# One helper of a fused attention and FFN block moved behind the attention core

## The chip, the cores and the metric

The kernel runs as one program on 8 NeuronCores of a Trainium2 chip. The metric is the device time in microseconds (us) of the slowest core. The engines are named as in the profile: PE is the matrix engine (PEld its weight load), DVE the vector engine, ACT the scalar engine, POOL the engine that issues the software DMAs here, and SP the engine that issues the DMA transposes. SPq, ACTq and POOLq are their queues of issued DMAs.

## The reference

A "macaron" block over x of shape (4, 4096, 1024), with 16 heads of 64:

```python
x = x + 0.5 * ffn(layernorm(x))
x = x + attn(layernorm(x))      # q, k with rotary embedding, |i - j| <= 128, softmax, Wo
x = x + 0.5 * ffn(layernorm(x))
# ffn: xr, xk mix x with the row before; sigmoid(xr @ W_r) * (relu(xk @ W_k)**2 @ W_v)
# rope: (x0, x1) -> (x0*c - x1*s, x1*c + x0*s), position modulo 256
```

Each core computes 2048 of the 16384 rows, with some rows of its neighbours added at either end.

## The kernel before

A core holds 20 tiles of 128 rows. Stage 1 is the first FFN, then comes the attention stage, then stage 4, the second FFN; x is spilled to the DRAM tensor `xscr` between them. The helper `P.op` appends an instruction with its semaphore waits to the list of one engine, so that every engine works through its own list in the order in which the Python code emits it, and nothing reorders them.

The attention stage is a loop over j = 1 to 19 in `emit_attn_stage`. One turn emits, in this order:

- `emit_qkv(j)`: 54 matmuls of 512 columns (L601, L606) into two PSUM banks in turn, and six copies on ACT (L625) into `qaug`, `kaug` and `vaug`. `qaug` and `kaug` exist once.
- `emit_qkv_tail(j)`, below called the tail: on ACT a square of q (L636), on DVE a sum per head (L642) and a maximum (L647), on ACT a logarithm and an exponential (L649, L651), on DVE the product that fills a 65th column of `qaug` (L655). This is the norm of q, which serves as stabilizer of the softmax. Then six DVE operations turn q and k in place (the rotary embedding, "rope": L667, L672 and L677, first for q, then for k). At the end SP transposes `qaug` into `qpl` and `kaug` into `kpl`.
- `emit_attn_core(j - 2)`, from j = 4 on: for each head three score matmuls (L709), an exponential on ACT (L718), a mask product on DVE (L723), and two heads later three matmuls with v (L736), evacuated by ACT or DVE in turn (L746, L751). Two PSUM banks hold scores. At its end DVE divides by the row sums (16 operations, L767), and SP transposes the result into `attnfm`.
- `emit_ln2(j + 1)`: the layer norm of the next tile: two passes over x on ACT (L204, L207), small operations on DVE and ACT, the scaled tile on DVE (L234), and a transpose on SP into `ln2fm`, for which the matmuls of `emit_qkv(j + 1)` wait.
- `emit_wo(j - 3)`, from j = 5 on: 18 matmuls (L789, L794) and two additions to x on DVE (L800), a store to `xscr` on POOL, and then the load of tile j + 5.

Turn j = 6 puts three large copies on POOL behind its store: W_r, W_k and W_v of the FFN are cast to 16 bits from DRAM to DRAM (`ffn16`). After turn 19 ACT issues three loads of these weights into `warena`, and then attention core 18, `emit_wo(17)` and `emit_wo(18)` close the stage.

Attention core j - 2 needs the transposes of tiles up to j - 1 only, not those of the tail of its own turn.

Of the kernel before, what the change touches and what calls it, by code (L numbers as in the profile page):

```python
# [11 lines left out]
ALU = mybir.AluOpType  # L12
AX = mybir.AxisListType
AP = bass.AP

NH, HD, DM = 16, 64, 1024
# [50 lines left out]
def build_nc():  # L67
# [34 lines left out]
    C_sb = sb("C_sb", [128, 2, DM], F16)  # L102
    S_sb = sb("S_sb", [128, 2, DM], F16)
    Cq_sb = sb("Cq_sb", [128, 2, DM], F16)
    Sq_sb = sb("Sq_sb", [128, 2, DM], F16)
# [15 lines left out]
    qsq_free = {0: []}  # L121
    qsq_waw = []
# [3 lines left out]
    P = Prog(nc)  # L126
# [16 lines left out]
    for hf, snw in ((0, "gw0a"), (1, "gw0b")):  # L143
        P.op("g", GD(warena[:, :, 512 * hf:512 * (hf + 1)],
                     AP(wr_d.tensor, 512 * hf, [[DM, 128], [128 * DM, 8], [1, 512]])),
             incs=[(snw, 16)])
# [5 lines left out]
    for nmw, (i, wd) in (("gw1", (1, wk_d)), ("gw2", (2, wv_d))):  # L152
# [5 lines left out]
         incs=[("gwo", 16)])  # L158
# [16 lines left out]
    v_cq = P.n("v")  # L175
# [329 lines left out]
    def emit_attn_stage(barrier, t_s1_mm, t_s1, s1_slots, s1_spill):  # L505
# [127 lines left out]

        def emit_qkv_tail(j):
            ev1, ev3 = qkv_ev[j]
            P.op("a", lambda a: a.activation(qsq[:, :],  # L636
                                             AP(qaug, 0, [[2 * DM, 128], [128, NH], [1, 64]]),
                                             AF.Square),
                 waits=[("s", ev1)] + qsq_free[0] + qsq_waw[:], incs=[("s", 1)])
            qsq_waw[:] = [("s", P.n("s"))]  # L640
            s_sq = P.n("s")
            P.op("v", lambda v: v.tensor_reduce(qm[:, 0, :],  # L642
                                                qsq[:, :].rearrange("p (h d) -> p h d", h=NH),
                                                AX.X, ALU.add),
                 waits=[("s", s_sq)], incs=[("v", 1)])
            qsq_free[0] = [("v", P.n("v"))]
            P.op("v", lambda v: v.tensor_scalar(qm[:, 0, :], qm[:, 0, :], 1e-12, None, ALU.max),  # L647
                 fence=True, incs=[("v", 1)])
            P.op("a", lambda a: a.activation(qm[:, 1, :], qm[:, 0, :], AF.Ln),  # L649
                 waits=[("v", P.n("v"))], incs=[("s", 1)])  # L650
            P.op("a", lambda a: a.activation(qm[:, 1, :], qm[:, 1, :], AF.Exp, scale=0.5),  # L651
                 waits=[("s", P.n("s"))], incs=[("s", 1)])
            s_nrm = P.n("s")
            with nc.allow_low_precision(reason="stabilizer M col; any nearby value is valid"):
                P.op("v", lambda v: v.tensor_tensor(  # L655
                    AP(qaug, 64, [[2 * DM, 128], [128, NH], [1, 1]]),
                    qm[:, 1, :], nkb2b[:, :], ALU.mult),
                    waits=[("s", s_nrm), ("v", v_pre)], incs=[("v", 1)])
            m_tok = P.n("v")
            par2 = (j + 1) % 2  # L660
            rope_tok = {}
            for which, aug, evw in (("q", qaug, ev1), ("k", kaug, ev3)):
                CC = Cq_sb if which == "q" else C_sb
                SS = Sq_sb if which == "q" else S_sb
                dv = AP(aug, 0, [[2 * DM, 128], [128, NH], [1, 64]])
                sv = AP(aug, 32, [[2 * DM, 128], [128, NH], [-32, 2], [1, 32]])
                P.op("v", lambda v, dv=dv, par2=par2, CC=CC: v.tensor_tensor(  # L667
                    t1[:, :].rearrange("p (h d) -> p h d", h=NH), dv, CC[:, par2, :]
                    .rearrange("p (h d) -> p h d", h=NH), ALU.mult),
                    waits=[("s", evw)] + ([("v", v_cq)] if which == "q" else []),  # L670
                    fence=(which == "k"), incs=[("v", 1)])
                P.op("v", lambda v, sv=sv, par2=par2, SS=SS: v.tensor_tensor(  # L672
                    t2[:, :].rearrange("p (h b d) -> p h b d", h=NH, b=2), sv,
                    SS[:, par2, :].rearrange("p (h b d) -> p h b d", h=NH, b=2), ALU.mult),
                    incs=[("v", 1)])
                w = [("s", s_sq)] if which == "q" else []
                P.op("v", lambda v, dv=dv: v.tensor_tensor(  # L677
                    dv, t1[:, :].rearrange("p (h d) -> p h d", h=NH),
                    t2[:, :].rearrange("p (h d) -> p h d", h=NH), ALU.add),
                    waits=w, fence=True, incs=[("v", 1)])  # L680
                rope_tok[which] = P.n("v")
            sn = f"yt{j % 4}"
            P.op("y", YT(qpl[:, j % 4, :, :], qaug[:, :]),
                 waits=[("v", rope_tok["q"]), ("v", m_tok)] + qpl_free[j % 4] +
                       ([(sn, P.n(sn))] if P.n(sn) > 0 else []),
                 incs=[(sn, 16)])
            P.op("y", YT(kpl[:, j % 4, :, :], kaug[:, :]),
                 waits=[("v", rope_tok["k"])] + kpl_free[j % 4], incs=[(sn, 16)])
            tr_tok[j] = (sn, P.n(sn))
# [129 lines left out]
        emit_ln2(1)  # L819
        for j in range(1, NT):  # L820
            emit_qkv(j)
            emit_qkv_tail(j)
            if QT0 <= j - 2 <= QT1:
                emit_attn_core(j - 2)
            if j + 1 < NT:
                emit_ln2(j + 1)
            if j == 1 or j == 19:
# [146 lines left out]
```

How the kernel before makes its waits and increments, by code:

```python
    def replay(self, q, eng, sems):  # L55
        for waits, build, incs in self.qs[q]:
            for s, v in waits:
                eng.wait_ge(sems[s], v)
            inst = build(eng)
            for s, a, _ in incs:
                if inst is None:
                    eng.sem_inc(sems[s], a)
                else:
                    inst.then_inc(sems[s], a)
```

## Time and profile before

| what | value |
|---|---|
| median of 2 runs | 1639.91 us (1636.69 to 1643.13) |
| the profiled execution, its own time | 1641.2 us |
| its span, slowest core (of 1620.9 to 1639.6) | 1639.6 us |
| PE busy | 1005.4 us, 61% |
| DVE busy | 610.3 us, 37% |
| ACT busy | 496.9 us, 30% |
| mean granted PE clock of the two dies | 0.771 and 0.743 |

No engine is busy all the time. The attention stage runs from about 486 us to about 1330 us of the span. In the rows below an instruction stands with its start and duration in us, and in brackets the idle time of its engine before it and what ended it.

### The profile page before, as it was taken

The page shows a single profiled execution, that of the slowest core. Times are in us where ns is not written, and L with a number is a line of the kernel's source. Part 1 is how long each engine was busy: PE and PEld are TensorE (multiplying, and loading weights), DVE is VectorE, ACT ScalarE, POOL GpSimd, SP SyncE. Part 2 cuts the span into 40 slices and gives each one's busy share as a digit, 9 for nine tenths or more (in the row PEclk, how much of TensorE's full clock was granted, in tenths as well). Part 3 has the DMA queues.
Part 4 walks back from the last instruction along what each step waited for, and adds up shares of the span by engine and source line. Part 5 has one row for each costly group of instructions (what it writes and reads, how often), then busy time and mean ns, then how long its engine had stood idle before and what let it go on. Part 6 is the DMA issues. An engine that isn't in the chain of part 4 may idle for free.

```text
span 1639.6 us, 18625 instructions; the slowest of 8 cores (1620.9 to 1639.6 us)
## 1 busy us (share of the span) xinstructions
PE 1005.4 (61%) x4645; PEld 427.0 (26%) x4645; DVE 610.3 (37%) x1674; ACT 496.9 (30%) x1054; POOL 38.4 (2%) x71
## 2 busy tenths in 40 slices
PE   0067842877816466662766766777766735767576
PEld 0023311332302122221333322333333312323222
DVE  1074403445311333332333333333344425445542
ACT  0133220432112233331333333333333422342231
POOL 1000000000010000000000000000000010000000
PEclk9987765777757766775777777777777766888878
DMA  9914495331381222269122232222222472333221
GB/s 149 208 33 102 104 114 118 89 90 52 90 275 33 44 47 40 65 92 165 31 61 65 65 63 53 54 65 52 52 52 52 107 238 48 90 95 86 71 71 65
DMA packets 224373, 141.16 MB, mean 86 GB/s; under 512 B 195472, under 2 KB 197648, under 8 KB 224080
## 3 DMA queue, kind: packets, MB, share of 16 engines
q1 hardware_dynamic: 193088, 48.25, 15.6%
q0 software_dynamic: 16592, 50.08, 15.1%
q10 hardware_dynamic: 14592, 41.63, 7.3%
q8 instruction: 45, 0.74, 0.2%
q14 instruction: 56, 0.46, 0.1%
HBM read 86.47 MB, written 39.85 MB: 77 GB/s over the span
## 4 chain that ended last, share of the span: by engine, by line
PE 36%; DVE 22%; DMA 18%; issue 9%; ACT 7%; SPq 4%; ACTq 1%; DVEq 1%; POOL 0%; POOLq 0%
PE pb L601 15%; PE pb L401 7%; DMA ln_fm_s<-ln_tm 7%; PE pb L709 4%; DMA ln2fm_s<-ln_tm 4%; SPq L137 4%; PE pb L736 3%; DVE xkm_s L346 3%; PE pb L369 3%; DVE xrm_s L341 3%; DMA kfm_s<-kpre_s 3%; PE pb L606 2%; DVE attn_tm_s L767 2%; ACT qsq L207 2%; DVE ln_tm L234 2%
## 5 line engine op out<-in xcount | busy, mean ns | idle before, releaser
L601 PE MATMUL pb<-warena,ln2fm_s 128*128 128x512 f16 x912 | 246.1, 418 | 165.0 <-DMA ln2fm_s<-ln_tm 165.0
L401 PE MATMUL pb<-warena,kfm_s 128*128 128x512 f16 x560 | 171.7, 476 | 155.7 <-DMA kfm_s<-kpre_s 154.6
L369 PE MATMUL pb<-warena,xrm_s 128*128 128x512 f16 x560 | 146.9, 423 | 107.9 <-DVE stats L211 50.3
L642 DVE TENSOR_REDUCE qm_s<-qsq 128x16 f32<-128x1024 f16 x19 | 23.2, 1220 | 401.3 <-ACT qsq L636 401.3
L709 PE MATMUL pb<-qpl_s,kpl_s 65*128 65x128 f16 x816 | 121.6, 286 | 73.4 <-ACT probsT_s L718 72.1
L601 PEld LDWEIGHTS pb<-warena,ln2fm_s 128*128 128x128 f16 x912 | 85.8, 104 | 292.4 <-issue 227.8
L718 ACT ACTIVATE probsT_s<-pb 128x384 bf16<-128x384 f32 x272 | 131.4, 490 | 50.6 <-PE pb L709 45.4
L369 PE MATMUL pb<-warena,xkm_s 128*128 128x512 f16 x560 | 140.2, 409 | 0.0
L736 PE MATMUL pb<-vaug_s,probsT_s 128*128 128x65 f16 x816 | 90.3, 236 | 78.2 <-DVE probsT_s L723 64.6
L401 PEld LDWEIGHTS pb<-warena,kfm_s 128*128 128x128 f16 x560 | 64.2, 117 | 259.9 <-issue 243.4
L379 ACT ACTIVATE r_sb_s<-pb 128x512 f16<-128x512 f32 x70 | 38.9, 595 | 274.0 <-DVE xr_sb L414 138.2
L204 ACT ACTIVATE ln_tm<-xr_sb 128x1024 f16<-128x1024 f32 x56 | 58.9, 1052 | 189.8 <-DVE xr_sb L414 56.4
L723 DVE TENSOR_TENSOR probsT_s<-probsT_s,gates_sb 128x256 bf16<-128x256 bf16 x272 | 76.4, 291 | 93.4 <-ACT probsT_s L718 66.7
L369 PEld LDWEIGHTS pb<-warena,xrm_s 128*128 128x128 f16 x560 | 58.3, 106 | 192.3 <-issue 164.8
L625 ACT ACTIVATE qaug_s<-pb 128x512 f16<-128x512 f32 x38 | 22.7, 597 | 228.0 <-PE pb L606 228.0
L789 PE MATMUL pb<-warena,attnfm_s 128*128 128x512 f16 x272 | 89.4, 488 | 3.8 <-DMA attnfm_s<-attn_tm_s 2.2
L736 PEld LDWEIGHTS pb<-vaug_s,probsT_s 128*128 128x128 bf16 x816 | 56.5, 117 | 121.4 <-issue 119.4
L709 PEld LDWEIGHTS pb<-qpl_s,kpl_s 65*128 65x128 f16 x816 | 62.9, 116 | 94.6 <-issue 83.5
L369 PEld LDWEIGHTS pb<-warena,xkm_s 128*128 128x128 f16 x560 | 57.9, 103 | 76.3 <-issue 44.0
L336 DVE TENSOR_TENSOR d_fm_s<-ln_fm_s 128x2048 f16<-128x2048 f16 x18 | 22.2, 1234 | 138.4 <-DMA ln_fm_s<-ln_tm 138.4
L409 DVE SCALAR_TENSOR_TENSOR t_sb_s<-pb,r_sb_s 128x512 f32<-128x512 f32 x70 | 47.0, 687 | 59.9 <-PE pb L401 59.9
L234 DVE TENSOR_SCALAR ln_tm<-xr_sb,stats 128x1024 f16<-128x1024 f32 x56 | 43.9, 810 | 48.7 <-ACT stats L228 48.7
(82 smaller groups left out, 842.4 us busy)
## 6 DMA issues: line engine op xcount, KB each, us to landing
xr_sb<-xscr POOLq DMA_DIRECT2D x36, 512.0 KB, 4.5
xr_sb<-x ACTq DMA_DIRECT2D x20, 512.0 KB, 5.4
xscr<-xr_sb ACTq DMA_DIRECT2D x19, 512.0 KB, 2.9
xscr<-xr_sb POOLq DMA_DIRECT2D x17, 512.0 KB, 2.9
out<-xr_sb ACTq DMA_DIRECT2D x16, 512.0 KB, 2.6
wqkv<-wqkv POOLq DMA_DIRECT2D x1, 6144.0 KB, 59.0
warena<-wqkv ACTq DMA_DIRECT2D x3, 2048.0 KB, 29.8
warena<-ffn ACTq DMA_DIRECT2D x3, 2048.0 KB, 21.5
```

Source lines behind the costliest of these rows:

```text
L137: YT = lambda o, i: (lambda y: y.dma_start(o, i, transpose=True))
L204: P.op("a", lambda a: a.activation(ln_tm[:, par, :], x_ap, AF.Copy, accum_out=sl(0)), waits=list(waits) + lnT_free[par] + stats_free.pop(s ...
L234: P.op("v", lambda v: v.tensor_scalar(ln_tm[:, par, :], x_ap, sl(2), sl(5), ALU.subtract, ALU.mult), waits=[("s", stok)] + list(waits) + l ...
L341: P.op("v", lambda v, c=c, gp=gp, o=o: v.scalar_tensor_tensor(xrm2[:, gp, c, o:o + 256], d_fm[:, c, o:o + 256], negmu[:, c:c + 1], ln_fm[: ...
L369: t.matmul(pb[bk][:, :], xm[:, gp, c, 128 * ti:128 * (ti + 1)], warena[:, c, woff + 512 * js:woff + 512 * (js + 1)], start=(c == 0), stop= ...
L401: P.op("t", lambda t, bk=bk, c=c, pp=pp, js=js: t.matmul(pb[bk][:, :], kfm[:, pp, c, :], warena[:, c, 2 * DM + 512 * js:2 * DM + 512 * (js ...
L601: P.op("t", lambda t, bk=bk, c=c, par=par, js=js: t.matmul(pb[bk][:, :], ln2fm[:, par, c, :], warena[:, c, 512 * js:512 * (js + 1)], start ...
L709: P.op("t", lambda t, sl=sl, h=h, ci=ci, par=par, bk=bk_sc: t.matmul(pb[bk][:, ci * 128:(ci + 1) * 128], AP(kpl, sl * NH * 128 + h * 128, ...
L718: P.op("a", lambda a, h=h, bk=bk_sc, hp=hp: a.activation(probsT[:, hp, :], pb[bk][:, 0:384], AF.Exp), waits=[("t", sc_tok[(i, h)])] + wp, ...
L723: P.op("v", lambda v, hp=hp, gi=gi: v.tensor_tensor(AP(probsT, hp * 384, [[4 * 384, 128], [256, 2], [1, 128]]), AP(probsT, hp * 384, [[4 * ...
L736: P.op("t", lambda t, sl=sl, h=h, ci=ci, hp=hp, bk=bk_pv: t.matmul(pb[bk][:, 0:65], AP(probsT, hp * 384 + ci * 128, [[4 * 384, 128], [1, 1 ...
L789: P.op("t", lambda t, bk=bk, c=c, par=par, js=js: t.matmul(pb[bk][:, :], attnfm[:, par, c, :], warena[:, c, 3 * DM + 512 * js:3 * DM + 512 ...
```

## The change

The tail is emitted behind the attention core of its turn instead of ahead of it. Inside the tail the rope of q and k comes first, and the norm of q is taken of the turned q (a turn leaves the norm as it is), so the square waits for the rope of q instead of for the copies from PSUM. No instruction is added or taken away.

```diff
         def emit_qkv_tail(j):
             ev1, ev3 = qkv_ev[j]
+            par2 = (j + 1) % 2
+            rope_tok = {}
+            for which, aug, evw in (("q", qaug, ev1), ("k", kaug, ev3)):
...
+                P.op("v", lambda v, dv=dv: v.tensor_tensor(
+                    dv, t1[:, :].rearrange("p (h d) -> p h d", h=NH),
+                    t2[:, :].rearrange("p (h d) -> p h d", h=NH), ALU.add),
+                    fence=True, incs=[("v", 1)])
+                rope_tok[which] = P.n("v")
             P.op("a", lambda a: a.activation(qsq[:, :],
                                              AP(qaug, 0, [[2 * DM, 128], [128, NH], [1, 64]]),
                                              AF.Square),
-                 waits=[("s", ev1)] + qsq_free[0] + qsq_waw[:], incs=[("s", 1)])
+                 waits=[("v", rope_tok["q"])] + qsq_free[0] + qsq_waw[:], incs=[("s", 1)])
...
-            par2 = (j + 1) % 2
-            rope_tok = {}
-            for which, aug, evw in (("q", qaug, ev1), ("k", kaug, ev3)):
...
             sn = f"yt{j % 4}"
             P.op("y", YT(qpl[:, j % 4, :, :], qaug[:, :]),
-                 waits=[("v", rope_tok["q"]), ("v", m_tok)] + qpl_free[j % 4] +
+                 waits=[("v", m_tok)] + qpl_free[j % 4] +
                        ([(sn, P.n(sn))] if P.n(sn) > 0 else []),
                  incs=[(sn, 16)])
...
         for j in range(1, NT):
             emit_qkv(j)
-            emit_qkv_tail(j)
             if QT0 <= j - 2 <= QT1:
                 emit_attn_core(j - 2)
+            emit_qkv_tail(j)
             if j + 1 < NT:
                 emit_ln2(j + 1)
```

On ACT, at the end of a turn and the start of the next, before (`vaug_s<-pb` is the last copy of the QKV product, `probsT_s` an exponential of the attention core, `ln_tm` and `qsq<-xr_sb` the two passes of the layer norm):

```order
L718 ACTIVATE probsT_s<-pb 128x384
L746 ACTIVATE attn_un_s<-pb 128x65
L204 ACTIVATE ln_tm,stats<-xr_sb 128x1024
L207 ACTIVATE qsq,stats<-xr_sb 128x1024
L227 ACTIVATE stats<-stats 128x1
L228 ACTIVATE stats<-stats 128x1
L625 ACTIVATE qaug_s<-pb 128x8x64 x2
L625 ACTIVATE kaug_s<-pb 128x8x64 x2
L625 ACTIVATE vaug_s<-pb 128x8x64 x2
L636 ACTIVATE qsq<-qaug_s 128x1024
L649 ACTIVATE qm_s<-qm_s 128x16
L651 ACTIVATE qm_s<-qm_s 128x16
```

The same stretch now (the code has moved by some lines: L717 and L745 are the old L718 and L746; L657, L670 and L672 are the square, logarithm and exponential of the tail):

```order
L717 ACTIVATE probsT_s<-pb 128x384
L745 ACTIVATE attn_un_s<-pb 128x65
L657 ACTIVATE qsq<-qaug_s 128x1024
L670 ACTIVATE qm_s<-qm_s 128x16
L672 ACTIVATE qm_s<-qm_s 128x16
L204 ACTIVATE ln_tm,stats<-xr_sb 128x1024
L207 ACTIVATE qsq,stats<-xr_sb 128x1024
L227 ACTIVATE stats<-stats 128x1
L228 ACTIVATE stats<-stats 128x1
L625 ACTIVATE qaug_s<-pb 128x8x64 x2
L625 ACTIVATE kaug_s<-pb 128x8x64 x2
L625 ACTIVATE vaug_s<-pb 128x8x64 x2
```

The three operations of the tail have moved from behind the copies of the QKV product to ahead of the layer norm's two passes.

On DVE, from the division at the end of an attention core to the masks of the next, before:

```order
L767 TENSOR_SCALAR attn_tm_s<-attn_un_s,zs_s 128x64 x16
L211 TENSOR_SCALAR stats<-stats 128x1
L218 TENSOR_SCALAR stats<-stats 128x1
L234 TENSOR_SCALAR ln_tm<-xr_sb,stats 128x1024
L800 TENSOR_TENSOR xr_sb<-pb,xr_sb 128x512 x2
L642 TENSOR_REDUCE qm_s<-qsq 128x16
L655 TENSOR_TENSOR qaug_s<-qm_s,nkb2b 128x16
L667 TENSOR_TENSOR t_s<-qaug_s,Cq_sb 128x1024
L677 TENSOR_TENSOR qaug_s<-t_s 128x16x64
L677 TENSOR_TENSOR kaug_s<-t_s 128x16x64
L723 TENSOR_TENSOR probsT_s<-probsT_s,gates_sb 128x2x128 x4
```

The same now (L766 is the old L767, L643 and L652 the old L667 and L677, L663 and L676 the old L642 and L655, L722 the old L723):

```order
L766 TENSOR_SCALAR attn_tm_s<-attn_un_s,zs_s 128x64 x16
L643 TENSOR_TENSOR t_s<-qaug_s,Cq_sb 128x1024
L652 TENSOR_TENSOR qaug_s<-t_s 128x16x64
L652 TENSOR_TENSOR kaug_s<-t_s 128x16x64
L663 TENSOR_REDUCE qm_s<-qsq 128x16
L676 TENSOR_TENSOR qaug_s<-qm_s,nkb2b 128x16
L211 TENSOR_SCALAR stats<-stats 128x1
L218 TENSOR_SCALAR stats<-stats 128x1
L234 TENSOR_SCALAR ln_tm<-xr_sb,stats 128x1024
L799 TENSOR_TENSOR xr_sb<-pb,xr_sb 128x512 x2
L722 TENSOR_TENSOR probsT_s<-probsT_s,gates_sb 128x2x128 x4
```

The whole tail now stands between the division and the statistics of the layer norm, and nothing stands ahead of the masks.

On SP, the last turns of the stage, before:

```order
L137 DMA_TRANSPOSE ln2fm_s<-ln_tm 128x8x128
L137 DMA_TRANSPOSE qpl_s<-qaug_s 128x16x128
L137 DMA_TRANSPOSE kpl_s<-kaug_s 128x16x128
L137 DMA_TRANSPOSE attnfm_s<-attn_tm_s 128x8x128 x2
L137 DMA_TRANSPOSE lnb_s<-ln_tm 128x8x128
```

And now:

```order
L137 DMA_TRANSPOSE ln2fm_s<-ln_tm 128x8x128
L137 DMA_TRANSPOSE attnfm_s<-attn_tm_s 128x8x128
L137 DMA_TRANSPOSE qpl_s<-qaug_s 128x16x128
L137 DMA_TRANSPOSE kpl_s<-kaug_s 128x16x128
L137 DMA_TRANSPOSE attnfm_s<-attn_tm_s 128x8x128
L137 DMA_TRANSPOSE lnb_s<-ln_tm 128x8x128
```

The transposes of the tail go behind that of the attention result, here and in every turn with an attention core.

## Rows read from the trace of the kernel before

**Rows 1.** Waits of the whole span: us in total, times, longest us.

```profile
PE pb L601 <- DMA ln2fm_s<-ln_tm: 165.0, 19, 36.2
...
PE pb L736 <- DVE probsT_s L723: 64.6, 21, 4.0
```

**Rows 2.** Timeline of turn 8, start of attention core: start, us, instruction [idle before <-releaser].

```profile
794.09 0.51 PE L709 MATMUL pb<-qpl_s,kpl_s 65*128 65x128 f16 x6
794.37 0.60 ACT L625 ACTIVATE vaug_s<-pb 128x512 f16<-128x512 f32 x1 [1.55 <-PE pb L606]
...
798.47 0.69 DVE L667 TENSOR_TENSOR t_s<-qaug_s,Cq_sb 128x1024 f16<-128x1024 f16 x1
...
802.06 0.69 DVE L677 TENSOR_TENSOR kaug_s<-t_s 128x1024 f16<-128x1024 f16 x1
...
803.21 0.33 PE L736 MATMUL pb<-vaug_s,probsT_s 128*128 128x65 f16 x3 [3.85 <-DVE probsT_s L723]
```

**Rows 3.** Timeline of turn 8, from the attention core's end to the next turn.

```profile
813.27 0.68 PE L736 MATMUL pb<-vaug_s,probsT_s 128*128 128x65 f16 x6 [0.70 <-DVE probsT_s L723]
...
817.63 0.15 DVE L211 TENSOR_SCALAR stats<-stats 128x1 f32<-128x1 f32 x1
...
820.33 1.23 SPq L137 DMA_TRANSPOSE ln2fm_s<-ln_tm  x1
...
823.41 3.48 PE L601 MATMUL pb<-warena,ln2fm_s 128*128 128x512 f16 x8 [3.75 <-DMA ln2fm_s<-ln_tm]
```

**Rows 4.** Timeline of attention core 18, which follows output product 16 at once.

```profile
1303.50 0.51 PE L709 MATMUL pb<-qpl_s,kpl_s 65*128 65x128 f16 x6
...
1315.49 0.33 PE L736 MATMUL pb<-vaug_s,probsT_s 128*128 128x65 f16 x3 [0.49 <-DVE attn_un_s L751]
```

**Rows 5.** Windows over attention core 18; then PE, PEld, DVE, ACT, POOL busy, PEclk, DMA, GB/s.

```profile
1303.40:1309.50 6.10, 4.76 (x51) 3.05 (x51) 3.25 (x12) 4.38 (x12) 0.53 (x1) 0.90 1.03 292
1309.50:1315.80 6.30, 5.42 (x48) 3.22 (x46) 3.06 (x14) 4.34 (x13) 0.00 (x0) 0.50 1.05 256
```

**Rows 6.** Timeline of turn 2, which has no attention core: tail, layer norm, next turn.

```profile
535.41 1.22 DVE L642 TENSOR_REDUCE qm_s<-qsq 128x16 f32<-128x1024 f16 x1 [21.59 <-ACT qsq L636]
...
537.70 0.23 DVE L655 TENSOR_TENSOR qaug_s<-qm_s,nkb2b 128x16 f16<-128x16 f32 x1 [0.79 <-ACT qm_s L651]
...
539.51 0.19 ACT L207 ACTIVATION_READ_ACCUMULATOR qsq<-xr_sb 128x1 f32 x1
...
542.23 2.02 SPq L137 DMA_TRANSPOSE kpl_s<-kaug_s  x1
...
544.76 1.52 SPq L137 DMA_TRANSPOSE ln2fm_s<-ln_tm  x1
```

**Rows 7.** Timeline of PE: first matmuls of turns 3, 8 and 15.

```profile
548.15 3.57 PE L601 MATMUL pb<-warena,ln2fm_s 128*128 128x512 f16 x8 [14.54 <-DMA ln2fm_s<-ln_tm]
...
779.90 3.19 PE L601 MATMUL pb<-warena,ln2fm_s 128*128 128x512 f16 x8 [28.89 <-DMA ln2fm_s<-ln_tm]
...
1088.42 1.89 PE L601 MATMUL pb<-warena,ln2fm_s 128*128 128x512 f16 x8 [3.19 <-DMA ln2fm_s<-ln_tm]
```

**Rows 8.** DMA issues of the page: operation, number, KB each, median us to landing.

```profile
ffn<-wv POOLq DMA_DIRECT2D x1, 2048.0 KB, 59.4
...
kpl_s<-kaug_s SPq DMA_TRANSPOSE x19, 4.7
```

**Rows 9.** Timeline beside the cast copies and the weight loads.

```profile
710.78 0.76 POOL L135 DMA_DIRECT2D ffn<-wv  x1
...
731.53 21.99 SPq L137 DMA_TRANSPOSE qpl_s<-qaug_s  x1
...
1296.75 6.57 ACTq L136 DMA_DIRECT2D warena<-ffn  x3
...
1301.19 1.35 SPq L137 DMA_TRANSPOSE attnfm_s<-attn_tm_s  x1
...
1318.01 3.57 PE L789 MATMUL pb<-warena,attnfm_s 128*128 128x512 f16 x8 [2.19 <-DMA attnfm_s<-attn_tm_s]
```

More of the change, by code:

```diff
@@ L635, in emit_qkv_tail @@
             ev1, ev3 = qkv_ev[j]
+            par2 = (j + 1) % 2
+            rope_tok = {}
+            for which, aug, evw in (("q", qaug, ev1), ("k", kaug, ev3)):
+                CC = Cq_sb if which == "q" else C_sb
+                SS = Sq_sb if which == "q" else S_sb
+                dv = AP(aug, 0, [[2 * DM, 128], [128, NH], [1, 64]])
+                sv = AP(aug, 32, [[2 * DM, 128], [128, NH], [-32, 2], [1, 32]])
+                P.op("v", lambda v, dv=dv, par2=par2, CC=CC: v.tensor_tensor(
+                    t1[:, :].rearrange("p (h d) -> p h d", h=NH), dv, CC[:, par2, :]
+                    .rearrange("p (h d) -> p h d", h=NH), ALU.mult),
+                    waits=[("s", evw)] + ([("v", v_cq)] if which == "q" else []),
+                    fence=(which == "k"), incs=[("v", 1)])
+                P.op("v", lambda v, sv=sv, par2=par2, SS=SS: v.tensor_tensor(
+                    t2[:, :].rearrange("p (h b d) -> p h b d", h=NH, b=2), sv,
+                    SS[:, par2, :].rearrange("p (h b d) -> p h b d", h=NH, b=2), ALU.mult),
+                    incs=[("v", 1)])
+                P.op("v", lambda v, dv=dv: v.tensor_tensor(
[3 more added lines that the diff above has]
+                rope_tok[which] = P.n("v")
             P.op("a", lambda a: a.activation(qsq[:, :],
@@ L659, in emit_qkv_tail @@
             m_tok = P.n("v")
-            par2 = (j + 1) % 2
-            rope_tok = {}
-            for which, aug, evw in (("q", qaug, ev1), ("k", kaug, ev3)):
[L663 to L681, printed above, removed]
             sn = f"yt{j % 4}"
             P.op("y", YT(qpl[:, j % 4, :, :], qaug[:, :]),
-                 waits=[("v", rope_tok["q"]), ("v", m_tok)] + qpl_free[j % 4] +
+                 waits=[("v", m_tok)] + qpl_free[j % 4] +
                        ([(sn, P.n(sn))] if P.n(sn) > 0 else []),
```

## The prediction

> **What bounds the kernel now.** I read the waits of the whole span first. PE, the engine with the most work, waits 165.0 us in 19 places for the transposed layer norm `ln2fm`, once per turn of the attention stage, and 64.6 us in 21 places for a mask product of DVE [rows 1]. So the stage is a chain that goes round through all engines, and I read one ordinary turn in the timeline, turn 8, which begins at 779.90 and ends at 823.41.
>
> It has two holes on PE. The first lies between the QKV product and the attention core: the first scores are issued at 794.09, but the first product with v comes at 803.21, because ACT does the square of the tail ahead of the exponentials and DVE does the sum and the six rope operations ahead of the masks [rows 2]. The core ends at 813.95. The second hole lies behind it: PE does the output product of an older tile and then stands 3.75 us until `ln2fm` has landed; the next turn starts at 823.41, 9.46 us after the core's end [rows 3].
>
> The change shortens the first hole and lengthens the second. The prediction is a count of both, and then of three places where a turn is not ordinary: turns 1 to 3, turn 7 and turn 19.
>
> **The first hole.** How fast a core goes when nothing stands ahead of it is shown in the trace of before by core 18, which comes directly behind output product 16: from its first scores at 1303.50 to its last product at 1315.82 it takes 12.3 us [rows 4]. PE's granted clock is 0.90 of full there for the first 6.1 us, close to the upper level of 2.4 GHz, and 0.50, the lower level, for the rest [rows 5]; I expect the same behind a QKV product. In turn 8 the first exponential can't start before the last copy of v ends at 794.97, which I count as 0.4 us more than in core 18 (estimate, between nothing and the 0.9 us from the first scores to that copy's end). So a core takes 12.7 us from its first scores, against 813.95 - 794.09 = 19.9 us now [rows 2, 3]. **Gain: 7.2 us a turn**, between 6.7 and 7.6.
>
> **The second hole.** I count from N, where the division ends and the next DVE operation starts: 817.63 in turn 8. From there it now takes 823.41 - 817.63 = 5.8 us to the next turn [rows 3]. With the tail in between:
> - the six rope operations: from 798.47 to 802.75, 4.3 us [rows 2]. The square of q on ACT needs only the rope of q and is done beside the rope of k, so it costs nothing; if it did not fit beside, it would be 1 us. The sum on DVE starts at N + 4.2;
> - from the start of that sum over maximum, logarithm and exponential to the end of the layer norm's two passes on ACT: 535.41 to 539.70 in turn 2, 4.3 us [rows 6]. These passes are now beside the division; behind the tail nothing hides them, since ACT works in order. N + 8.5;
> - from the statistics to the transpose's issue: 817.63 to 820.33, 2.7 us, and 0.1 us for the hand-over from ACT [rows 3]. N + 11.3. SP has by then had two double transposes: it can issue the first when the 65th column is written (537.93 - 535.41 = 2.5 us behind the start of the sum, so at about N + 6.9), each takes 2.0 us or a little more [rows 6], and so SP is free between N + 11.1 and N + 11.5. I add 0.2 us;
> - from the issue to the first matmul: 548.15 - 544.76 = 3.4 us, in turn 2, where the transpose also comes right behind the two double ones [rows 6, 7]. N + 14.9.
>
> That is 14.9 - 5.8 = **9.1 us more a turn**, so a turn grows by 1.9 us. The bounds: 0.5 us if SP is free early and the landing takes 3.1 us as in turn 8, and 4 us if the four transposes in a row disturb one another. The holes that lie behind an attention core are those of turns 4 to 18; without turn 7 that makes 14 x 1.9 = **+26.6 us** (7 to 56).
>
> **The clock at the head of a turn.** The first eight matmuls of a turn took 3.57 us behind a hole of 14.5 us, 3.19 us in turn 8 and 1.89 us in turn 15, where the clock had stayed up [rows 7]. With a hole of 13 us ahead of each turn I expect nearly always the slow value. I take 0.4 us a turn, **+6 us** in 15 turns; the bounds are nothing and 0.55 us a turn (8 us).
>
> **Turns 1 to 3** have no attention core, so the tail stays where it was. But its rope now comes first in DVE's list, and DVE is idle there (21.59 us ahead of the sum [rows 6]), so the rope runs beside the QKV product. The layer norm's statistics then wait for ACT alone (539.70) and not for the rope. I count 2.0 us less each, **-6 us** in all; nothing to 7 us.
>
> **Turn 7** lies under the cast copies of the FFN weights. The last is issued at 710.78 and takes 59.4 us to land; beside it a double transpose, of 2 us in a quiet turn, holds SP for 21.99 us [rows 8, 9], and turn 8 starts only at 779.90, behind 28.89 us of waiting [rows 7], about 69 us after that issue. The copies wait on POOL behind the store of turn 6, which waits for the layer norm on DVE; so they move together with the start of turn 7. The transposes of attention result, q, k and layer norm still all need the copies to be over before they get through. Both orders reach turn 8 some 69 us behind the issue: **0 us**, between -21 (the copies are over before the tail's transposes) and +10.
>
> **Turn 19.** Now attention core 18 starts at 1303.50, right behind the output product. The three weight loads are issued on ACT from 1296.75 on [rows 4, 9]. In the new order ACT reaches them behind the exponential of tail 19, at about N + 6.3, and SP issues the two double transposes of that tail at N + 6.9 and N + 9: in the middle of the loads, and core 18 can't start without them. In quiet turns the transpose of k lands 4.7 us after its issue [rows 8]. Beside these loads the single transpose issued at 1301.19 let PE start only at 1318.01, 16.8 us later [rows 9]. For the double one I take 25 us (estimate: one and a half times the single, between the quiet 4.7 and twice 16.8), so that core 18 starts at N + 34 instead of at N + 2.5 (N is about 1301 in turn 19). Core 17 has brought 7.2 us: 31.5 - 7.2 = **+24 us**, between +4 and +33. The output product behind core 18 and stage 4 follow at the same distance as now.
> The Trainium skill, DMA: Bandwidth & Descriptors, section "Issuing engines are not separate DMA queues", says that DMAs issued from different engines run on the same 16 DMA engines and interleave. The trace agrees by the 16.8 us just named. Were SP's and ACT's transfers independent, this term would be +4 and the sum 20 us lower.
>
> **The sum.** 26.6 + 6 - 6 + 0 + 24 = +50.6 us on the profiled execution's own 1641.2 us: 1691.8. The median of the runs lies 1.3 us lower, at 1639.9: **1690.5 us**, 3.1% slower. About 2% is what a measurement of this kernel can tell from no change, and that is 1607 to 1673.
>
> **The rivals.**
> - *The loads are missed.* Place: turn 19. If the k transpose gets through beside the weight loads, or its bytes are taken ahead of them, the term is +4 instead of +24: 1670 us, within 2%. For it: it is issued only 2.7 us behind the first load, the other one 4.4 us. Against it: all of that one's 16.8 us.
> - *Not slower: the transposes pass both floods.* If a transpose of the tail waits for neither the casts in turn 7 (-21) nor the loads in turn 19 (-20), and so those large copies are hidden under the attention core, the time is 1690 - 41 = 1649; with the seam at its low bound of 0.5 us, another 20 us off, 1629 us. It decides at the casts' landing: they must be in 38 us after their issue instead of 59.4, since attention core 5 ends by then. For it: no double transpose runs beside the casts in their first 40 us now. Against it: the 59.4 us were mostly without one as well.
> - *The casts hurt more.* Four transposes in a row meet the casts in turn 7, and each of them may take its 20 us: +20, 1711 us. Against it: the copies are over by then for half of them.
> - *The seam is worse than counted.* If the transposes that follow one another add 2 us a turn: +30, 1720 us. Against it: turn 2 shows three of the four in a row at 3.4 us.
> - *The change does nothing to the first hole*, since ACT and not the tail limits the core. Then 1690 + 15 x 7.2 = 1798 us. Core 18 speaks against it; I give it nothing.
>
> **How the numbers follow.** The forecast with its small terms has 0.57, the loads missed 0.11, both floods passed 0.09, the casts 0.11, the seam 0.09; 0.03 are left for what I don't see, 0.02 of them on the fast side. Faster by over 2%: 0.02. Within 2%: the loads missed and most of the passed floods, 0.19. Slower: 0.79. The terms have about +-15 us from the seam and +-10 us from turn 19, and the range takes in the missed loads and the casts' or the seam's rival: 1660 to 1722 us.
>
> **What would show it.** Right: a hole of about 13 us ahead of the QKV product in place of 3.7, about 9 us from the division's end to the layer norm's statistics; the waits of PE for masks nearly gone; attention cores of about 12.7 us; core 18 some 25 to 30 us later behind core 17, with PE waiting for `kpl`. Wrong: a core that still takes 16 us or more; a turn below 44 us; or a turn 8 that starts at another distance than 69 us from the cast's issue.

## The result and the profile after

The changed kernel takes 1701.57 us (median of 11 runs) against 1642.2 us (median of 10 runs of the kernel before beside them). The ratio is 1.0353, 95% interval 1.0326 to 1.038: slower by 58 us, where 50.6 us were forecast. The time lies inside the stated range.

The page of the profile after. The execution took 1709.14 us, and the page shows core 0, the slowest. First the span, then the groups that answer to [rows 1]:

```profile
span 1707.6 us, 18587 instructions; the slowest of 8 cores (1672.1 to 1707.6 us)
...
L601 PE MATMUL pb<-warena,ln2fm_s 128*128 128x512 f16 x912 | 262.0, 439 | 295.6 <-DMA ln2fm_s<-ln_tm 295.6
...
L708 PE MATMUL pb<-qpl_s,kpl_s 65*128 65x128 f16 x816 | 115.8, 274 | 49.5 <-DMA kpl_s<-kaug_s 29.4
...
L735 PE MATMUL pb<-vaug_s,probsT_s 128*128 128x65 f16 x816 | 86.2, 228 | 18.9 <-DVE attn_un_s L750 7.9
```

PE's wait for `ln2fm` has grown from 165.0 to 295.6 us; its wait ahead of the products with v, 64.6 us for the mask alone [rows 1], is 18.9 us from all causes; and one wait of 29.4 us for the k transpose is new. These are the two holes and turn 19 of the prediction.

In that execution, as in some others, the cores of one die had a lower clock (0.72 against 0.754 to 0.759), core 0 among them; the ratios, and the times given for the experiments, leave out the executions that this made clearly longer. So I compare core 6 of it (clock 0.754, span 1683.4 us) with the profile of before, which is also of core 6 (clock 0.748). First the windows over attention core 15, in turn 17: its first 6.1 us, the rest, and the whole (length; PE, PEld, DVE, ACT, POOL busy; granted PE clock, DMA share, GB/s):

```profile
1207.00:1213.10 6.10, 4.50 (x46) 2.96 (x45) 2.32 (x9) 4.57 (x12) 0.00 (x0) 0.80 0.00 1
1213.10:1219.80 6.70, 5.89 (x53) 3.60 (x51) 3.31 (x14) 4.70 (x14) 0.00 (x0) 0.50 0.01 2
1207.00:1219.80 12.80, 10.39 (x97) 6.56 (x96) 5.62 (x23) 9.27 (x25) 0.00 (x0) 0.64 0.01 2
```

Then the timeline of core 6, from the end of that attention core to the layer norm's transpose (start, us, instruction, idle before):

```profile
1219.56 0.32 PE L735 MATMUL pb<-vaug_s,probsT_s 128*128 128x65 f16 x3 [0.40 <-DVE attn_un_s L750]
...
1223.57 0.68 DVE L643 TENSOR_TENSOR t_s<-qaug_s,Cq_sb 128x1024 f16<-128x1024 f16 x1
...
1225.86 1.06 ACT L657 ACTIVATE qsq<-qaug_s 128x1024 f16<-128x1024 f16 x1 [6.38 <-DVE qaug_s L652]
...
1227.76 1.21 DVE L663 TENSOR_REDUCE qm_s<-qsq 128x16 f32<-128x1024 f16 x1
...
1231.86 0.19 ACT L207 ACTIVATION_READ_ACCUMULATOR qsq<-xr_sb 128x1 f32 x1
1232.15 0.15 DVE L211 TENSOR_SCALAR stats<-stats 128x1 f32<-128x1 f32 x1 [1.87 <-ACT qsq L207]
1232.41 0.16 DVE L213 TENSOR_TENSOR stats<-stats 128x1 f32<-128x1 f32 x1
1232.41 2.44 SPq L137 DMA_TRANSPOSE kpl_s<-kaug_s  x1
...
1235.05 1.54 SPq L137 DMA_TRANSPOSE ln2fm_s<-ln_tm  x1
```

The attention core takes 12.8 us from its first scores; the kernel before needed 19.9 [rows 2, 3]. From N, here 1223.57, the sum starts at N + 4.2, the two passes of the layer norm end at N + 8.5 and its transpose is issued at N + 11.5, as in the prediction to 0.1 us. Over turns 5 to 18 of this core (without turn 7) the issue comes at N + 11.7 on average, because the transpose of k holds SP for 2.3 to 3.5 us and not for 2.0.

The beginning of the next turn on PE of the same core:

```profile
1239.23 3.57 PE L601 MATMUL pb<-warena,ln2fm_s 128*128 128x512 f16 x8 [12.85 <-DMA ln2fm_s<-ln_tm]
1242.74 0.60 PE L606 MATMUL pb<-wqkvb_sb,ones 1*128 1x512 f16 x1
1243.27 2.66 PE L601 MATMUL pb<-warena,ln2fm_s 128*128 128x512 f16 x8
1245.86 0.39 PE L606 MATMUL pb<-wqkvb_sb,ones 1*128 1x512 f16 x1
1246.18 1.90 PE L601 MATMUL pb<-warena,ln2fm_s 128*128 128x512 f16 x8
```

The transpose lands so that PE starts 4.2 us after its issue; I had taken 3.4. This turn is one of the longest in that: the same turns lie between 3.4 and 4.4 us, 3.7 on average. And the lower clock lasts into the second group of eight matmuls (2.66 us), where I had counted only the first. The QKV product takes 15.6 us here, against 14.6 in most turns before.

Turn 19 on core 6 after:

```profile
1325.24 7.48 ACTq L136 DMA_DIRECT2D warena<-ffn  x3
...
1325.91 10.60 SPq L137 DMA_TRANSPOSE qpl_s<-qaug_s  x1
...
1336.65 10.08 SPq L137 DMA_TRANSPOSE kpl_s<-kaug_s  x1
1351.22 0.80 PE L708 MATMUL pb<-qpl_s,kpl_s 65*128 65x128 f16 x6 [29.34 <-DMA kpl_s<-kaug_s]
```

The weight loads and the two double transposes go side by side, each transpose holds SP for some 10 us instead of 2, and PE waits 29.34 us.

What each term measures, from the first matmuls of the turns (start of turn 5 to start of turn 19, without turn 7) and the ends of the attention cores, on core 6 and as the mean of all eight:

| term | forecast | core 6 | mean of 8 cores |
|---|---|---|---|
| attention core, each | -7.2 | -7.3 (20.0 to 12.8) | -7.3 |
| core's end to next turn, each | +9.1 | +9.6 (9.5 to 19.1) | +9.6 |
| QKV product, each | +0.4 | +0.75 | +0.7 |
| a turn | +2.3 | +3.05 (43.92 to 46.97) | +3.1 |
| hole ahead of turns 2 to 4 | -2.0 each | -2.0 (14.5 to 12.5) | |
| turn 7, start to start | 0 | -4.9 (69.55 to 64.64) | -0.6 (68.8 to 68.1) |
| turn 19, to the start of core 18, with core 17 | +24 | +22.3 (29.6 later, less 7.3) | +23.2 |

With the means, 14 turns of 3.1, less 6 and 0.6, plus 23.2 make 60 us, against 58 by the ratio.

Single cores scatter around this. Turn 7 is 4.9 us shorter on core 6, but up to 5.9 us longer on others (66.9 to 72.2 us before, 64.6 to 73.0 after), so core 6 alone shows no effect of the new order there. Core 6 needs 52.5 us more than before from the start of turn 1 to attention core 18 (817.1 to 869.6), the mean of the eight cores 63.2. Part of the difference is in the QKV products of turns 1 to 3: together they are 2.4 us shorter on core 6 and longer on core 0, so they follow the clock of the execution and not the order. The whole span of core 6 is 43.8 us longer, less than its attention stage, since its turn 1 starts 4.8 us sooner and what follows core 18 takes 3.9 us less, in code that the change leaves alone; why was not traced.

### The profile page after: what moved, and what is told of

It reads as the page before. It is cut to its first block, busy times and chain, and to the rows that moved or that the text cites. A ratio compares the mean times of both kernels' runs of the same rounds, so it can differ in the third digit from the quotient of the medians.

```text
span 1707.6 us, 18587 instructions; the slowest of 8 cores (1672.1 to 1707.6 us)
## 1 busy us (share of the span) xinstructions
PE 1049.5 (61%) x4645; PEld 431.5 (25%) x4645; DVE 613.7 (36%) x1674; ACT 496.2 (29%) x1054; POOL 38.4 (2%) x71
## 4 chain that ended last, share of the span: by engine, by line
PE 36%; DVE 20%; DMA 18%; issue 9%; ACT 8%; SPq 6%; ACTq 2%; DVEq 1%; POOL 0%; POOLq 0%
PE pb L601 15%; DMA ln_fm_s<-ln_tm 7%; PE pb L401 7%; SPq L137 6%; PE pb L708 5%; DMA ln2fm_s<-ln_tm 4%; PE pb L735 4%; DVE xkm_s L346 3%; PE pb L369 3%; DVE xrm_s L341 3%; ACT qsq L207 3%; DVE attn_tm_s L766 3%; DMA kfm_s<-kpre_s 3%; PE pb L606 2%; ACT probsT_s L717 2%
## 5 line engine op out<-in xcount | busy, mean ns | idle before, releaser
L601 PE MATMUL pb<-warena,ln2fm_s 128*128 128x512 f16 x912 | 262.0, 439 | 295.6 <-DMA ln2fm_s<-ln_tm 295.6
L722 DVE TENSOR_TENSOR probsT_s<-probsT_s,gates_sb 128x256 bf16<-128x256 bf16 x272 | 79.5, 292 | 453.3 <-ACT probsT_s L717 413.8
L369 PE MATMUL pb<-warena,xrm_s 128*128 128x512 f16 x560 | 157.7, 446 | 100.0 <-DVE stats L211 52.3
L369 PE MATMUL pb<-warena,xkm_s 128*128 128x512 f16 x560 | 153.1, 436 | 0.0
L717 ACT ACTIVATE probsT_s<-pb 128x384 bf16<-128x384 f32 x272 | 131.4, 490 | 67.4 <-PE pb L708 58.6
L708 PE MATMUL pb<-qpl_s,kpl_s 65*128 65x128 f16 x816 | 115.8, 274 | 49.5 <-DMA kpl_s<-kaug_s 29.4
L401 PEld LDWEIGHTS pb<-warena,kfm_s 128*128 128x128 f16 x560 | 64.6, 117 | 249.0 <-issue 249.0
L735 PE MATMUL pb<-vaug_s,probsT_s 128*128 128x65 f16 x816 | 86.2, 228 | 18.9 <-DVE attn_un_s L750 7.9
L788 PE MATMUL pb<-warena,attnfm_s 128*128 128x512 f16 x272 | 93.0, 503 | 1.8 <-DMA attnfm_s<-attn_tm_s 1.3
L735 PEld LDWEIGHTS pb<-vaug_s,probsT_s 128*128 128x128 bf16 x816 | 52.1, 111 | 62.9 <-issue 58.5
L341 DVE SCALAR_TENSOR_TENSOR xrm_s<-d_fm_s,negmu,ln_fm_s 128x256 f16<-128x256 f16 x144 | 58.6, 479 | 2.1
## 6 DMA issues: line engine op xcount, KB each, us to landing
warena<-ffn ACTq DMA_DIRECT2D x3, 2048.0 KB, 17.6
```

Of the source, the lines that this page charges most:

```text
L341: P.op("v", lambda v, c=c, gp=gp, o=o: v.scalar_tensor_tensor(xrm2[:, gp, c, o:o + 256], d_fm[:, c, o:o + 256], negmu[:, c:c + 1], ln_fm[: ...
L369: t.matmul(pb[bk][:, :], xm[:, gp, c, 128 * ti:128 * (ti + 1)], warena[:, c, woff + 512 * js:woff + 512 * (js + 1)], start=(c == 0), stop= ...
L401: P.op("t", lambda t, bk=bk, c=c, pp=pp, js=js: t.matmul(pb[bk][:, :], kfm[:, pp, c, :], warena[:, c, 2 * DM + 512 * js:2 * DM + 512 * (js ...
L601: P.op("t", lambda t, bk=bk, c=c, par=par, js=js: t.matmul(pb[bk][:, :], ln2fm[:, par, c, :], warena[:, c, 512 * js:512 * (js + 1)], start ...
L708: P.op("t", lambda t, sl=sl, h=h, ci=ci, par=par, bk=bk_sc: t.matmul(pb[bk][:, ci * 128:(ci + 1) * 128], AP(kpl, sl * NH * 128 + h * 128, ...
L717: P.op("a", lambda a, h=h, bk=bk_sc, hp=hp: a.activation(probsT[:, hp, :], pb[bk][:, 0:384], AF.Exp), waits=[("t", sc_tok[(i, h)])] + wp, ...
```

## The experiments

Each was run beside the kernel before on the same chip; the differences in us are worked out from the ratios to it, times 1640.

**The inner order.** The old tail, behind the core:

```diff
-            emit_qkv_tail(j)
             if QT0 <= j - 2 <= QT1:
                 emit_attn_core(j - 2)
+            emit_qkv_tail(j)
```

> The tail stands behind the attention core as in the changed kernel, but inside it the old order is kept (norm of q first, rope after it). The theory of the seam: what counts is the chain from the end of the division to the issue of the layer norm's transpose. With the old inner order the square runs on ACT beside the division, the sum starts at N, the rope ends at N + 6.7 us with the layer norm's two ACT passes beside it, and the transpose is issued at N + 9.5 instead of N + 11.5 us. That is 2.0 us less a turn in 15 turns, 6 us more in turns 1 to 3, some 3 us less in turn 19: about 27 us below the changed kernel, near 1675. Rival (the seam is set by the transposes in SP's queue and their landing, the inner order is idle detail): within 8 us of the changed kernel, near 1700.

Measured: 1668.6 us, ratio 1.0189 (1.0135 to 1.0243), 27 us below the changed kernel and 31 us above the kernel before. The timeline of its core 0, turn 18:

```profile
1249.60 1.06 ACT L636 ACTIVATE qsq<-qaug_s 128x1024 f16<-128x1024 f16 x1
1251.10 2.69 DVE L767 TENSOR_SCALAR attn_tm_s<-attn_un_s,zs_s 128x64 f16<-128x64 f32 x16
1253.71 1.22 DVE L642 TENSOR_REDUCE qm_s<-qsq 128x16 f32<-128x1024 f16 x1
...
1260.74 0.15 DVE L211 TENSOR_SCALAR stats<-stats 128x1 f32<-128x1 f32 x1
...
1264.20 1.23 SPq L137 DMA_TRANSPOSE ln2fm_s<-ln_tm  x1
```

The square runs beside the division, the statistics start 7.0 us behind N (1253.71) and not 8.6, and the transpose goes out at N + 10.5 (N + 9.6 on average of this core's turns). A turn takes 44.6 us instead of 47.1, as the mean of the eight cores. The inner order that the change brings is thus the wrong one for the place where it puts the tail: rope first makes the square wait for DVE. The chain through the engines sets the seam; in this turn SP's second double transpose (3.06 us, 2.4 on average) adds most of another 1 us.

**The inner order alone.** The changed tail, put back ahead of the core:

```diff
+            emit_qkv_tail(j)
             if QT0 <= j - 2 <= QT1:
                 emit_attn_core(j - 2)
-            emit_qkv_tail(j)
```

> Only the inner order changes: the tail stays ahead of the attention core, but its rope comes first and can run on DVE beside the QKV product, since it waits only for the copies of q and k. The theory of the first hole: it is the sum of what ACT and DVE do between the last copy of v and the first mask. 4.1 us of it are the rope and go, so a core takes 15.8 us from its first scores instead of 19.9, and nothing is added to the seam. 15 turns of 4.1 us, 6 us in turns 1 to 3, less what turn 7 keeps because of the cast copies: 60 to 68 us below the kernel before, near 1578. Rival (the copies from PSUM or ACT's square alone set the hole, DVE's rope is beside them already): within 10 us of before, 1632 to 1642. A second rival says that the position behind the core would be needed to gain anything.

Measured: 1570.2 us, ratio 0.958 (0.9543 to 0.9618), 69 us below before. Its timeline on core 7, turn 14:

```profile
1010.44 1.05 ACT L657 ACTIVATE qsq<-qaug_s 128x1024 f16<-128x1024 f16 x1
1011.59 1.22 DVE L663 TENSOR_REDUCE qm_s<-qsq 128x16 f32<-128x1024 f16 x1 [3.09 <-ACT qsq L657]
...
1013.63 0.87 ACT L717 ACTIVATE probsT_s<-pb 128x384 bf16<-128x384 f32 x2
1013.88 0.23 DVE L676 TENSOR_TENSOR qaug_s<-qm_s,nkb2b 128x16 f16<-128x16 f32 x1 [0.79 <-ACT qm_s L672]
...
1014.29 0.68 DVE L722 TENSOR_TENSOR probsT_s<-probsT_s,gates_sb 128x256 bf16<-128x256 bf16 x2 [0.19 <-ACT probsT_s L717]
```

The first mask stands directly behind the norm's product; the six rope operations of [rows 2] are gone from between. A core takes 16.1 us from its first scores, 3.9 us less than before. So one half of the change, the inner order, gains 69 us by itself, and the place behind the core takes it away and 58 more. The two halves don't add: the place costs 31 us with the old inner order and 127 us with the new one, and the new inner order gains 69 us ahead of the core and loses 27 us behind it.

**The weight loads of turn 19.**

```diff
-                 waits=([("t", t_qkv_last[0]), ("gf6", g_ffn16[0])] if i == 0 else []),
+                 waits=([("t", t_qkv_last[0]), ("gf6", g_ffn16[0]), tr_tok[19]] if i == 0 else []),
```

> The changed kernel, but the three weight loads of turn 19 wait until the transposes of tail 19 have landed. The theory of turn 19: core 18 stands 29 us waiting for its k transpose because that shares the DMA engines with the loads; without them it lands 14 us after the division's end instead of 34, core 18 starts 20 us sooner, and the kernel gains 15 to 20 us: 1682 to 1687. Rival (the loads have to be moved some time anyway, and now hold up the transpose of core 18's result and the start of the last stage): the gain is given back, within 5 us of 1701.

Measured: 1687.8 us, ratio 1.0299 (1.0249 to 1.035), 9 us below the changed kernel by the ratios and 14 by the medians: less than expected. The timeline of its core 4:

```profile
1338.71 4.87 SPq L137 DMA_TRANSPOSE kpl_s<-kaug_s  x1
1345.43 5.80 ACTq L136 DMA_DIRECT2D warena<-ffn  x3
1345.82 0.80 PE L708 MATMUL pb<-qpl_s,kpl_s 65*128 65x128 f16 x6 [13.10 <-DMA kpl_s<-kaug_s]
1351.38 0.87 ACT L717 ACTIVATE probsT_s<-pb 128x384 bf16<-128x384 f32 x2 [15.25 <-issue]
```

PE waits 13.10 us instead of 29.34, so the theory of the collision holds; core 18 starts 16.7 us sooner behind core 17 (mean of the eight cores). But issuing the three loads keeps ACT for 5.8 us, and the core's first exponential stands behind them: 5.6 us between the first scores and that exponential were not in my count. The difference, 11 us, lies between the two figures above. The intervals of the two ratios overlap a little, so it is the trace more than the time that decides here.

**The order on SP.** The two double transposes behind that of the layer norm:

```diff
+            tail_y[j] = (m_tok, rope_tok)
+        def emit_tail_y(j):
...
             if j + 1 < NT:
                 emit_ln2(j + 1)
+            emit_tail_y(j)
```

> The changed kernel, but SP issues the layer norm's transpose ahead of the tail's two double transposes. The theory of the landing: in the changed kernel the first matmul of a turn comes 4.2 us after the issue of that transpose, against 3.1 us before, because the transpose of k is still being moved. With the new order it is 3.1 us again, and the issue needs not wait for SP, 0.2 us: 1.3 us less in 15 turns, about 19 us below the changed kernel, near 1682. The tail's transposes then land some 5 us into the QKV product, whose copies into qaug wait for them; that may cost up to 1 us a turn. Rival (those copies wait for the late transposes and the QKV product stalls for want of PSUM banks by more than is gained): 1701 or more, up to 1730.

Measured: 1743.3 us, ratio 1.0629 (1.0595 to 1.0664): the rival. Its timeline on core 7, SP at the end of turn 12, then ACT and PE in the QKV product of turn 13:

```profile
1055.92 1.22 SPq L137 DMA_TRANSPOSE ln2fm_s<-ln_tm  x1
1057.33 2.62 SPq L137 DMA_TRANSPOSE qpl_s<-qaug_s  x1
1060.10 3.63 SPq L137 DMA_TRANSPOSE kpl_s<-kaug_s  x1
```

```profile
1067.36 1.08 ACT L626 ACTIVATE qaug_s<-pb 128x512 f16<-128x512 f32 x2 [12.61 <-DMA kpl_s<-kaug_s]
...
1068.10 1.89 PE L602 MATMUL pb<-warena,ln2fm_s 128*128 128x512 f16 x8 [2.58 <-ACT qaug_s L626]
```

The landing did get shorter: turn 13 starts at 1059.03, 3.1 us after the issue. But `qaug` exists once, the copies wait for the late transposes, and PE stands 2.58 us inside the QKV product. In turn 7 the late transposes meet the cast copies: ACT waits 55 us at one copy, and that turn takes 91.7 us instead of 68.1. From a core's end to the next turn 0.9 us is gained (19.2 to 18.3), while the QKV product takes 2.8 us longer (15.2 to 18.0; means of the eight cores).

**The clock.** 48 extra matmuls behind each output product; they write a bank that nobody reads, and the output is unchanged.

```diff
+            if 5 <= j < NT - 1:
+                for dd in range(48):
+                    P.op("t", lambda t: t.matmul(
+                        pb[3][:, :], warena[:, 0, 3 * DM:3 * DM + 128],
+                        warena[:, 0, 3 * DM:3 * DM + 512], start=True, stop=True),
+                        waits=(bank_free[3] if dd == 0 else []))
```

> The changed kernel, with 48 extra matmuls of 512 columns behind each output product from turn 5 to 18 that write a PSUM bank nobody reads (their result is not used). They fill most of PE's hole ahead of the next turn. The theory of the clock: the QKV product takes 15.4 us instead of 13.0 only because its first matmuls run at the lower granted clock behind the hole; with PE busy it takes 13.0 to 13.3, which is 2.2 us less in 13 turns: about 28 us below the changed kernel, near 1673. Rival (extra work on all cores brings the granted clock of the whole die down, or the extra matmuls run past the hole): 1701 or more.

Measured: 1679.5 us, ratio 1.025 (1.0168 to 1.0333), 17 us below the changed kernel with an interval as wide as the gain. Two windows of its core 0, the hole ahead of turn 19 and the QKV product behind it (the last figures are the granted clock, the DMA share and GB/s):

```profile
1266.50:1279.30 12.80, 10.59 (x49) 4.62 (x48) 5.51 (x13) 3.52 (x9) 0.53 (x1) 1.00 0.69 129
1279.40:1292.30 12.90, 12.87 (x54) 4.75 (x54) 0.00 (x0) 2.99 (x5) 0.00 (x0) 1.00 0.03 10
```

With the hole filled the clock stays at its upper level, 2.4 GHz, and the product takes 12.96 us. Not in all turns: leaving out turn 8, behind the cast copies, 67 of the 104 products on the eight cores take 12.96 us and 37 some 14.5. The 48 matmuls leave a rest of the hole. Turns 13 and 14 of core 0:

```profile
999.33 1.89 PE L601 MATMUL pb<-warena,ln2fm_s 128*128 128x512 f16 x8 [1.91 <-DMA ln2fm_s<-ln_tm]
...
1046.24 3.49 PE L601 MATMUL pb<-warena,ln2fm_s 128*128 128x512 f16 x8 [4.49 <-DMA ln2fm_s<-ln_tm]
```

All 51 products behind a rest of up to 2.6 us are fast, all 26 behind one of 3.04 us or more are slow, and between these both occur. On average the product is 1.4 us shorter than in the changed kernel, and a turn 1.2 us. So these matmuls give back about 1.4 us a turn, not 2.2.

**The cast copies.** In the kernel with the inner order alone, and in the changed kernel:

```diff
-            if j == 6:
-                for ii, wd in enumerate((wr_d, wk_d, wv_d)):
+            if j in (6, 9, 12):
+                ii, wd = {6: (0, wr_d), 9: (1, wk_d), 12: (2, wv_d)}[j]
```

> The kernel with only the inner order changed (1570 us), and the three cast copies put into turns 6, 9 and 12 instead of all into turn 6. The theory of turn 7: 25 us of its length are the wait for the three copies, which last 60 us together, longer than a turn. One copy of 20 us ends beside the QKV product and the attention core, before the layer norm's transpose is wanted. So the wait of 29 us in turn 7 goes and none comes: 22 to 25 us less, 1545 to 1549. Rival (each copy holds up the tail's or the layer norm's transposes of its own turn by 8 us or more): 1565 to 1575.

> The changed kernel with the cast copies in turns 6, 9 and 12 instead of all in turn 6. In its trace turn 7 takes 64.6 us on a core whose other turns take 47.0, so the copies cost it 17.6 us, 8 less than the 25.5 they cost in the kernel before. Expected: that goes, 16 to 18 us below the changed kernel, near 1684. Rival (in the changed kernel each copy is still under way when the row of four transposes is issued): within 8 us of 1701.

Measured: 1532.6 and 1539.5 us, ratio 0.9362 (0.9268 to 0.9455, wide since it rests on these two of four executions), some 36 us below the inner order alone, more than the 22 to 25 expected; and 1675.6 us, ratio 1.0217 (1.02 to 1.0234), 22 us below the changed kernel, where 16 to 18 were expected. In the second, SP's double transposes of turn 7 on core 5 take no longer than elsewhere:

```profile
748.50 1.94 SPq L137 DMA_TRANSPOSE qpl_s<-qaug_s  x1
750.59 2.26 SPq L137 DMA_TRANSPOSE kpl_s<-kaug_s  x1
753.04 1.80 SPq L137 DMA_TRANSPOSE ln2fm_s<-ln_tm  x1
```

Before the change the transposes of q and k took 21.99 and 19.10 us there, on core 6. The traces agree with both gains: as the mean of the eight cores turn 7 takes 45.9 us instead of 68.1 in the changed kernel, and 38.7 instead of 71.4 in the one with the inner order alone. The expectations had taken the cost of the copies from the wait in the kernel before (25 us) and from core 6 alone (17.6 us).

**The tail split.** Rope and the transpose of k ahead of the core, norm and the transpose of q behind the layer norm:

```diff
             emit_qkv(j)
+            emit_qkv_tail(j)           # rope of q and k, transpose of k
             if QT0 <= j - 2 <= QT1:
                 emit_attn_core(j - 2)
-            emit_qkv_tail(j)
             if j + 1 < NT:
                 emit_ln2(j + 1)
+            emit_norm(j)               # square to 65th column, transpose of q
```

> The tail is split. Its rope and the transpose of k are emitted ahead of the attention core and run beside the QKV product; the norm of q and the transpose of q come behind the next tile's layer norm. Then nothing stands ahead of the core and nothing ahead of the layer norm. The theory of two holes: a core takes 12.8 us from its first scores as in the changed kernel, and the next turn starts about 9.5 us behind the core's end as in the kernel before. The transpose of q lands some 10 us behind the division's end, 1 us later than the copies of the next QKV product want it, which costs about 0.5 us. A turn of 37.5 us instead of 44.1 (before) or 47 (changed); with 5 us less in each of turns 1 to 3 and no gain in turn 7: 1525 to 1540. Rival (the transpose behind the layer norm stalls the QKV product by 2 to 4 us a turn and meets the cast copies, as it did when both double transposes were issued late): 1565 to 1600.

Measured: 1528.2 us, ratio 0.935 (0.9255 to 0.9445), 107 us below the kernel before. Its timeline on core 7 at the end of turn 17:

```profile
1092.40 0.15 DVE L211 TENSOR_SCALAR stats<-stats 128x1 f32<-128x1 f32 x1
...
1095.10 1.22 SPq L137 DMA_TRANSPOSE ln2fm_s<-ln_tm  x1
...
1097.73 1.36 SPq L137 DMA_TRANSPOSE qpl_s<-qaug_s  x1
...
1098.21 3.12 PE L602 MATMUL pb<-warena,ln2fm_s 128*128 128x512 f16 x8 [3.55 <-DMA ln2fm_s<-ln_tm]
```

The statistics stand directly behind the division, and PE waits 3.55 us as in [rows 3]. The attention core takes 12.8 us. Turn 17 has neither hole: 35.6 us from 1062.62 to 1098.21; the turns take 36.7 us on average.

**All together.** The split tail, the casts in turns 7, 10 and 13 behind the landing of the previous tail's transposes, and the weight loads issued by SP behind tail 19's:

```diff
+            if j in (7, 10, 13):
+                ii, wd = {7: (0, wr_d), 10: (1, wk_d), 13: (2, wv_d)}[j]
+                P.op("g", GD(ffn16[:, ii * DM:(ii + 1) * DM], wd),
+                     waits=[tr_tok[j - 1]], incs=[("gf6", 16)])
...
-            P.op("a", AD(warena[:, :, i * DM:(i + 1) * DM],
+            P.op("y", AD(warena[:, :, i * DM:(i + 1) * DM],
...
-                 waits=([("t", t_qkv_last[0]), ("gf6", g_ffn16[0])] if i == 0 else []),
+                 waits=([("t", t_qkv_last[0]), ("gf6", g_ffn16[0]), tr_tok[19]] if i == 0 else []),
```

> The split tail (1528 us), with the three cast copies in turns 7, 10 and 13, each waiting for the transposes of the tail before it, and with the three weight loads of the end issued by SP behind the landing of tail 19's transposes instead of by ACT. By the theory of the two floods turn 7 loses its 30 us of waiting, and core 18 starts about 10 us behind output product 16 instead of 24: some 40 us less in all, 1485 to 1495. Rival (the copies still meet a transpose that is wanted, three times instead of once, and the loads now hold up the last transpose and the start of the last stage): 1510 to 1528.

Measured: 1487.8 us, ratio 0.9071 (0.9049 to 0.9094), 152 us below the kernel before and the fastest of all. On its core 6 turn 7 takes 37.0 us (674.67 to 711.63), and core 18 starts 4.8 us behind output product 16, where the kernel with the split tail alone needed 23.8 (its core 7).

## Why the prediction was right, point by point

- *The first hole closes: right.* 7.3 us against 7.2. Core 18 of the kernel before was the right model: the others now take 12.8 us, with the clock at 0.80 of full in the first 6.1 us and at 0.50, the lower level, behind it; core 18 had 0.90 and 0.50 [rows 5].
- *The second hole: right in its working, 0.5 us short in size.* The chain over DVE and ACT, from N to the end of the two passes, holds to 0.1 us. Two later terms were mis-sized. The transpose of k holds SP for 2.6 us on average and not for 2.0, so the issue comes at N + 11.7 and not at N + 11.5. From the issue to the first matmul 3.4 us were taken from turn 2, where three transposes come in a row; behind four it is 3.7 us on average, up to 4.4. The run with the transposes turned round goes back to 3.1 us, so it is the transposes ahead that lengthen it.
- *The clock: right in kind, about half in size.* I had counted the first eight matmuls only; the lower clock lasts into the next eight. The extra matmuls show more of the effect: 12.96 us at the upper clock against 15.2 us on average.
- *Turns 1 to 3: right*, -2.0 us each in the holes.
- *Turn 7: right*, in size: -0.6 us as the mean of the eight cores, and turn 8 starts 68.5 us behind the last cast issue on average, against 68.4 before. In the working one statement was wrong, that the transpose of the attention result needs the copies to be over: on core 6 it is issued at 737.24, 31.5 us behind the last cast issue, and holds SP for 1.74 us. The one of q behind it takes 17.27 us, so the turn ends with the copies all the same. Spreading the casts shows that they still cost the changed kernel 22 us.
- *Turn 19: right in sum*, +22.3 against +24 us, *by luck in its parts*. I let SP issue the transpose of k at N + 9 and gave it 25 us to land. On core 6 (N is 1319.03) the transpose of q holds SP for 10.60 us first, the one of k is issued at N + 17.6 and PE starts 14.6 us later. Both together give N + 32.2 against the N + 34 forecast. The loads and the transposes collide: the wait falls from 29.34 to 13.10 us when the loads are held back. The section of the Trainium skill named in the prediction (DMA: Bandwidth & Descriptors, "Issuing engines are not separate DMA queues") is borne out by the same rows. That run also shows a cost that neither theory had, ACT's own 5.8 us of issue.
- *The rivals.* No transpose of the tail passed the floods, and the loads were not missed. A turn was worse than counted by 0.8 us with the clock, not by 2.

The terms add up to 60 us as the mean of the eight cores, against 50.6 forecast and 58 measured by the ratio; nearly all that the forecast lacks is the 0.8 us in each of 14 turns.

## What to carry to other kernels

Moving work from ahead of a stage to behind it only moves a hole when every engine works in order and the stage behind waits for the same engines: count from the last shared instruction to the next needed one, on both sides. The gain here lay in splitting the moved block by what its parts wait for: the part whose inputs come early goes beside the product before, the part that nobody needs soon goes behind what is needed first. And check for a bulk copy beside every transposing DMA that someone waits for. In this kernel holding the copy back, or cutting it into pieces shorter than a turn, gave 9 to 36 us.

## What was not expected of the hardware

Three weight loads held ACT for 5.8 to 7.5 us at their issue. In the run that held them back an exponential waited behind them; in the kernel before, the same 6.57 us [rows 9] ended at 1303.32, just ahead of the scores at 1303.50, and cost nothing that shows. And a rest of the hole of only 3 us ahead of the QKV product went with the lower clock at its head (14.5 us instead of 13.0), while one of 2.6 us did not; what decides between these two stays open. The attention core loses the upper clock without standing still: in its second part PE is busy for 5.89 of 6.70 us and has 0.50 of the clock.
